# An attention layer on one core: the softmax shift's rest on another engine, q and k loaded in three runs of rows, and the first band edges ahead of the output

## The reference

```python
x = x + attention(layernorm(x))     # 16 heads of 16, Wq, Wk, Wv, Wo
x = x + ffn(layernorm(x))           # ternary weights, a low-rank side path, relu squared
# attention:
attend = (abs(i - j) <= 128) | (i < 1) | (j < 1)
logits = where(attend, q @ k.T / 4, -inf)
out = softmax(logits) @ v @ Wo.T
```

## Time and profile before

| | |
|---|---|
| time, median of 3 runs | 1136.79 us (1133.0 to 1143.12) |
| the profiled execution: its own time, its span | 1132.38 us, 1130.5 us |
| busy over the span: TensorE, VectorE, ScalarE, GpSimd | 93%, 83%, 68%, 61% |
| TensorE's mean granted clock | 0.984 of full |
| exps (1591), 512 | 394.4 us busy, 140.9 idle before, 137.8 of it for score banks |
| tiles read (1644), 1024 | 402.2 us busy, 66.6 idle before, 62.7 of it for TensorE |
| band edges (1417), 256 | 270.5 us busy, 10.6 idle before |
| outputs (1456), 64 | 39.8 us busy, 122.9 idle before, 100.3 of it for the reciprocal |
| value products (1529), 2816 | 223.0 us busy, 23.9 idle before, 20.2 of it for the band edges |
| score products (1507), 5632 | 242.1 us busy, 19.4 idle before, 13.5 of it for the shift rows' transfer |

### The profile page before, as it was taken

The page is one execution under the profiler, slowest core; times in us unless marked ns, Lnnn a source line. Parts: engine busy times, 40 slices in busy tenths (PEclk is TensorE's granted clock), DMA queues, the critical chain, the costliest instruction groups (busy, mean ns, idle before and its releaser), DMA issues. The chain is left out here.

```text
span 1130.5 us, 40183 instructions
## 1 busy us (share of the span) xinstructions
PE 1056.5 (93%) x16091; PEld 789.1 (70%) x16091; DVE 939.7 (83%) x3233; ACT 772.8 (68%) x1321; POOL 690.4 (61%) x916
## 2 busy tenths in 40 slices
PE   9999998998989989898998999889999999999998
PEld 8888884455555555455555566458888888898887
DVE  7899856997989988897888999657888788878885
ACT  7999984676777777776777777745655456545654
POOL 3665558486778877876787877853443344433443
PEclk9999998899999999999999999989999999999999
DMA  6999898457556566564566664230411122112201
GB/s 202 298 303 281 268 252 202 110 130 149 132 134 145 113 133 159 129 141 107 133 147 143 149 143 103 59 115 1 129 58 57 57 87 81 57 57 66 67 20 38
DMA packets 189707, 145.69 MB, mean 129 GB/s; under 512 B 61240, under 2 KB 189264, under 8 KB 189520
## 3 DMA queue, kind: packets, MB, share of 16 engines
q1 hardware_dynamic: 189520, 143.12, 49.0%
HBM read 91.32 MB, written 50.95 MB: 126 GB/s over the span
## 5 line engine op out<-in xcount | busy, mean ns | idle before, releaser
L1591 ACT ACTIVATE a_weights<-e_psum 128x1024 f32<-128x1024 f32 (+1 forms) x512 | 394.4, 809 | 140.9 <-PE e_psum L1507 137.8
L1644 DVE CUSTOM_DVE_ANT_0 a_masked<-e_psum,band 128x290 f32<-128x290 f32 (+8 forms) x1024 | 402.2, 444 | 66.6 <-PE e_psum L1482 62.7
L1417 POOL TENSOR_SCALAR_AFFINE_SELECT a_weights<-a_weights 128x1024 f32<-128x1024 f32 x256 | 270.5, 1091 | 10.6 <-ACT a_weights L1591 10.5
L1869 POOL TENSOR_TENSOR f_square<-f_relu 128x512 f32<-128x512 f32 x128 | 146.2, 1143 | 209.4 <-ACT f_relu L1858 192.1
L1507 PE MATMUL e_psum<-e_q,e_k 128*32 128x256 bf16 (+2 forms) x5632 | 242.1, 281 | 19.4 <-DMA e_q<-a_shift 13.5
L1482 PE MATMUL e_psum<-e_k,e_q 96*32 96x290 bf16 (+2 forms) x4096 | 233.9, 290 | 14.6 <-DVE a_max L1644 6.9
L1529 PE MATMUL e_psum<-a_weights,a_v 128*17 128x384 f32 (+2 forms) x2816 | 223.0, 398 | 23.9 <-POOL a_weights L1417 20.2
L1507 PEld LDWEIGHTS e_psum<-e_q,e_k 128*32 128x32 bf16 x5632 | 129.9, 97 | 115.1 <-ACT a_weights L1591 39.1
L1482 PEld LDWEIGHTS e_psum<-e_k,e_q 96*32 96x32 bf16 x4096 | 113.2, 98 | 86.1 <-DVE a_max L1644 54.9
L1825 PE MATMUL e_psum<-w_w_t,f_square_hi 128*128 128x256 f32 x512 | 129.4, 287 | 5.7 <-DVE f_square_lo L1915 5.7
L1827 PE MATMUL e_psum<-w_w_t,f_square_lo 128*128 128x256 f32 x512 | 126.7, 282 | 0.0
(11 more groups left out here) (218 smaller groups left out, 1898.1 us busy)
## 6 DMA issues: line engine op xcount, KB each, us to landing
k_parts<-p_k_parts SPq DMA_DIRECT2D x48, 258.0 KB, 4.2
e_k<-k_parts SPq DMA_DIRECT2D x64, 193.5 KB, 3.6
e_k<-k_parts SPq DMA_DIRECT2D x192, 64.5 KB, 3.3
q_parts<-p_q_parts SPq DMA_DIRECT2D x48, 256.0 KB, 4.9
e_q<-q_parts SPq DMA_DIRECT2D x64, 192.0 KB, 3.7
e_q<-q_parts SPq DMA_DIRECT2D x192, 64.0 KB, 3.3
v_ones<-p_va SPq DMA_DIRECT2D x16, 544.0 KB, 5.4
p_x<-in_x SPq DMA_DIRECT2D x16, 512.0 KB, 6.2
```

The source lines that it names most:

```text
L1417: pool.affine_select(out=blocks, in_=blocks, compare_op=ALU.is_ge, fill=0.0, base=0, pattern=[[0, NQ // 2 * HEAD_COLS // P // CUT_STEP], [ ...
L1591: act.activation(pe_w[:, us.upar, lo:hi], score[c % 2][:], ACT.Exp).then_inc(s_exp, 1)
L1644: dve.tensor_tensor_reduce(out=masked[:, place + lo:place + hi], in0=bank[:, lo:hi], in1=band[:, lo:hi], scale=1.0, scalar=NEG, op0=ALU.ad ...
L1869: pool.tensor_tensor(sh.r2[:, j % 4, :], sh.r[:, j % 4, :], sh.r[:, j % 4, :], ALU.mult).then_inc(self.s_sq, 1)
```

## The change

- **Rest.** The difference between the maxima and their HIGH is taken by GpSimd, as the first thing in a second step, instead of by VectorE behind tile 4. It is no longer negated: q's three rows now hold the maximum itself, and k's rows of ones hold minus ones.
- **HIGH** is copied by ScalarE ahead of the step's first exp instead of behind it.
- **LOW** comes ahead of key 0's products on GpSimd instead of behind them.
- **Band edges.** The first two (the first half of the weights, both sides) come ahead of the output, the other two stay behind it.
- **q and k.** In DRAM the part is now the outermost dimension, ahead of the row within a head, so that runs of rows in a tile's order of slots are single transfers: `RUNS` has three for each tile (48, 32 and 16 rows) where there were four (48 and three of 16). For that the columns of the turned Q and K weights are ordered otherwise, and they are copied in halves.

```diff
@@ -47,7 +47,7 @@
 
-TWO_ONES = float(np.array([0x3F803F80], np.uint32).view(np.float32)[0])
+MINUS_ONES = float(np.array([0xBF80BF80], np.uint32).view(np.float32)[0])
 DMA = 16
@@ -56,7 +56,7 @@
 SLOTS = 6
-SINGLES = ((MID, HIGH, HIGH), (HIGH, MID, HIGH))
+RUNS = (((0, 3), (0, 2), (0, 1)), ((0, 3), (1, 3), (2, 3)))
 SLOT_ROWS = SLOTS * HD
@@ -272,6 +272,16 @@
     sem[1] = start + 3
+
+
+def head_columns(w, m):
+
+    return w[:, m * P:(m + 1) * P].rearrange("p (d i h) -> p i h d", d=HD, h=NQ)
+
+
+def head_rows(w, m):
+
+    return w.rearrange("p (h m i d) -> p m i h d", h=NQ, m=KT, d=HD)[:, m]
 
@@ -394,12 +404,12 @@
                 if q := at(LP):
-                    rows = q_dram[bass.ds(q.g, 1)].rearrange("a i d s h m t -> (a i d) s (h m t)")
+                    rows = q_dram[bass.ds(q.g, 1)].rearrange("a s d i h m t -> (a d i h) s (m t)")
                     for part, done in ((HIGH, s_high), (MID, s_mid), (LOW, s_low)):
                         sp.wait_ge(done, q.g * 4 + KT)
                         sp.dma_start(rows[:, PLACE[0][part]], q_parts[:, q.par, :, PLACE[0][part]]
                                      ).then_inc(s_qout[q.par], DMA)
-                    rows = k_dram[bass.ds(q.g, 1)].rearrange("a i d s h m t -> (a i d) s (h m t)")
+                    rows = k_dram[bass.ds(q.g, 1)].rearrange("a s d i h m t -> (a d i h) s (m t)")
                     sp.wait_ge(s_gap, q.g * KT + KT)
@@ -598,9 +608,9 @@
                 for k in range(KT):
-                    ins = act.activation(wt_hi[:, w, k].rearrange("p (i d h) -> p i h d", d=HD, h=NQ),
-                                         w_bank[w][:, k * D:(k + 1) * D].rearrange("p (h i d) -> p i h d", d=HD, h=NQ),
-                                         ACT.Copy)
+                    for m in range(KT):
+                        ins = act.activation(head_columns(wt_hi[:, w, k], m), head_rows(w_bank[w][:, k * D:(k + 1) * D], m),
+                                             ACT.Copy)
                 ins.then_inc(s_whi, 1)
...
@@ -1220,7 +1230,7 @@
 
-    LOADS = 1 + len(SINGLES[0])
+    LOADS = len(RUNS[0])
 
@@ -1233,15 +1243,15 @@
         m, i = u.hq // 2, u.hq % 2
-        places = [(1, k_dram[b * GB + c:b * GB + c + 1, i, :, :, :, m], self.kt[u.hq][:, :, c * KGT:(c + 1) * KGT])
+        places = [(1, k_dram[b * GB + c:b * GB + c + 1, :, :, i, :, m], self.kt[u.hq][:, :, c * KGT:(c + 1) * KGT])
                   for b, c in self.chunks_of(u)]
-        places += [(0, q_dram[u.g:u.g + 1, i, :, :, :, m], self.qw[u.q])]
+        places += [(0, q_dram[u.g:u.g + 1, :, :, i, :, m], self.qw[u.q])]
         for which, src, dst in places:
-            src = src.rearrange("a d s h t -> (a d) s h t")
-            sp.dma_start(dst[0:PARTS * HD], src.rearrange("d s h t -> (d s) h t")).then_inc(landed, DMA)
-            for n, part in enumerate(SINGLES[which]):
-                sp.dma_start(dst[(PARTS + n) * HD:(PARTS + n + 1) * HD], src[:, PLACE[which][part]]
-                             ).then_inc(landed, DMA)
+            src, first = src.rearrange("a s d h t -> (a s d) h t"), 0
+            for start, stop in RUNS[which]:
+                count = stop - start
+                sp.dma_start(dst[first * HD:(first + count) * HD], src[start * HD:stop * HD]).then_inc(landed, DMA)
+                first += count
 
...
@@ -1420,12 +1430,20 @@
                 um, us, uo = at(L_SHIFT), at(L_SCORE), at(L_OUT)
+                if um and um.last:
+                    pool.wait_ge(s_high, um.pair + 1)
+                    wait(pool, s_low, um.pair)
+                    pool.tensor_tensor(rest[:], mt[:], shift[:, um.ppar, HIGH, :], ALU.subtract).then_inc(s_rest, 1)
                 if uo:
                     pool.wait_ge(s_turned, uo.n + 1)
                     pool.tensor_tensor(den[:, uo.upar], turned[:, uo.upar, :, HD], p0[:, uo.p0], ALU.add
                                        ).then_inc(s_den, 1)
                     pool.tensor_tensor(num[:, uo.upar], turned[:, uo.upar, :, 0:HD], t0[:, uo.n % 3], ALU.add
                                        ).then_inc(s_num, 1)
+                if um and um.last:
+                    pool.wait_ge(s_mid, um.pair + 1)
+                    pool.tensor_tensor(shift[:, um.ppar, LOW, :], rest[:], shift[:, um.ppar, MID, :], ALU.subtract
+                                       ).then_inc(s_low, 1)
                 if us:
@@ -1437,16 +1455,15 @@
                         p0[:, us.p0].unsqueeze(2).broadcast_to([P, SUBS, HD]), ALU.mult).then_inc(s_t0, 1)
-                if um and um.last:
-                    pool.wait_ge(s_mid, um.pair + 1)
-                    pool.tensor_tensor(shift[:, um.ppar, LOW, :], rest[:], shift[:, um.ppar, MID, :], ALU.subtract
-                                       ).then_inc(s_low, 1)
                 if um:
                     pool.wait_ge(s_tile_read, um.n * TILES + TILES)
                     wait(pool, s_p0, um.n - 1)
                     pool.tensor_tensor(d0[:, um.upar].rearrange("p (t j) -> p t j", j=QUADS), key0_scores(um),
                                        mx[:, um.ppar, um.upar * TILES:(um.upar + 1) * TILES].rearrange("p (t j) -> p t j", j=QUADS), ALU.subtract
                                        ).then_inc(s_d0, 1)
+                if us:
+                    cut(us, 0, 0)
+                    cut(us, 0, 1)
                 if uo:
@@ -1458,8 +1475,6 @@
                         feed.norm.power(pool, Group(0))
-                    cut(us, 0, 0)
-                    cut(us, 0, 1)
                     cut(us, 1, 0)
...
@@ -1582,6 +1597,10 @@
                     feed.act_o_high(act, Group(1))
+                if um and um.last:
+                    act.wait_ge(s_m, um.pair + 1)
+                    wait(act, s_row[um.ppar], um.phalf * DMA * SHIFT_ROWS)
+                    act.activation(shift[:, um.ppar, HIGH, :], mt[:], ACT.Copy).then_inc(s_high, 1)
                 for c in range(CHUNKS):
@@ -1589,10 +1608,6 @@
                         act.activation(pe_w[:, us.upar, lo:hi], score[c % 2][:], ACT.Exp).then_inc(s_exp, 1)
-                    if um and um.last and c == 0:
-                        act.wait_ge(s_m, um.pair + 1)
-                        wait(act, s_row[um.ppar], um.phalf * DMA * SHIFT_ROWS)
-                        act.activation(shift[:, um.ppar, HIGH, :], mt[:], ACT.Copy, scale=-1.0).then_inc(s_high, 1)
                     if um and um.last and c == 2:
@@ -1626,12 +1641,6 @@
                 for j in range(TILES):
-                    if um and um.last and j == 4:
-                        dve.wait_ge(s_high, um.pair + 1)
-                        wait(dve, s_low, um.pair)
-                        dve.scalar_tensor_tensor(out=rest[:], in0=mt[:], scalar=-1.0,
-                                                 in1=shift[:, um.ppar, HIGH, :], op0=ALU.mult, op1=ALU.subtract
-                                                 ).then_inc(s_rest, 1)
                     if ux:
@@ -2068,8 +2077,8 @@
 def layer(nc, x, wq, wk, wv, wo, fast_b, w_fc, w_proj, u, v, gate, out):
-    q_dram = nc.dram_tensor("q_parts", [G, UPG // KT, HD, PARTS, NQ, KT, GT], BF16, kind="Internal").ap()
-    k_dram = nc.dram_tensor("k_parts", [G, UPG // KT, HD, PARTS, NQ, KT, KGT], BF16, kind="Internal").ap()
+    q_dram = nc.dram_tensor("q_parts", [G, PARTS, HD, UPG // KT, NQ, KT, GT], BF16, kind="Internal").ap()
+    k_dram = nc.dram_tensor("k_parts", [G, PARTS, HD, UPG // KT, NQ, KT, KGT], BF16, kind="Internal").ap()
     va_dram = nc.dram_tensor("v_ones", [N, VROW], F32, kind="Internal").ap()
```

14 lines of the change are left out of this document (7 added, 7 removed).

## The result

| | before | changed |
|---|---|---|
| time, median | 1137.92 us (4 runs, 1133.0 to 1143.12) | 1105.6 us (4 runs, 1103.48 to 1110.43) |
| ratio | | 0.9721, 95% interval 0.9665 to 0.9778 |
| profiled execution: time, span | 1132.38, 1130.5 us | 1110.43, 1108.7 us |
| the 58 steps of the loop | 493.41 us | 464.04 us |

The kernel became 2.8% faster, and 1104 was forecast. The profiled execution of the changed kernel is the slowest of its four. Timed again twice, beside new runs of the kernel before, the changed kernel had a ratio of 0.9718 (0.966 to 0.9777) and 0.9757 (0.97 to 0.9813).

A forecast was written before the change was run, and what follows sets the result against it. A cycle through GpSimd's band edges and VectorE's reciprocal was taken to set the 8.27 us step, late shift rows second. Terms -19.3 - 3 + 4 - 11 + 0.3 = -29.0 gave 1104 us, range 1076 to 1126 (8 in 10).

The forecast's parts named there:

- the ring: Attention loop: band edges, value products, VectorE's reciprocal, GpSimd's output, edges again; 8.27 us, said to set the step's length.
- The edges, -19.3 us: Attention loop: two of four edges leave the cycle, giving back TensorE's 19.3 us of waiting for edges; bounds 0 and -46.
- 7.81: Attention loop: TensorE's busy time per quiet step in us, taken as the next limit once the edges move.
- the first rival: Attention loop: TensorE's busy time is no floor, steps fall to 7.5 us; -53, 1081 us, chance 0.17.
- Low earlier and fewer transfers, -11 us: Shift rows into q: LOW a microsecond sooner, six transfers a unit instead of eight; 80% of 13.2 us saved.
- Now it is late for all three: SyncE in the kernel before: still issuing the odd unit's loads when the shift rows are ready; some 1.0 us a unit saved.
- At most two steps over 9 us, and no clock below full: Attention loop: a sign that would show the forecast right, long steps and lowered TensorE clock nearly gone.
- +0.3: Kernel's start: Q and K weights copied in twice as many halves, costing 0 to +1 us.
- Rest off VectorE, -3: Attention loop: rest moves to GpSimd, saving half of TensorE's 6.6 us wait for VectorE's reads; 0 to -6.6.
- HIGH ahead, +4: ScalarE in the loop: first exp waits for turned maxima and HIGH's copy, about 0.2 us in 29 steps; 0 to +5.
- The last rival: ScalarE: HIGH ahead of the first exp makes a new cycle, +43 us, sum +12, 1146 us; slower, chance 0.08.
- That the rows come late all the same: Shift rows: transfers queue on DMA engines, not SyncE, so only -18 us, some 1115 us; chance 0.14.

The follow-up runs named there:

- E: Kernel before with only the first two band edges moved ahead of GpSimd's output: 1130.2 us, ratio 0.9937.
- S: Kernel before with only the shift's chain changed (rest on GpSimd, HIGH ahead of the first exp, LOW ahead of key 0's products): 1134.97 us, ratio 0.9994.
- the paced kernel: Changed kernel with SyncE holding back every odd step's loads until that step's third exp: 1109.05 us, ratio 0.9732 to the kernel before.
- L: Kernel before with only q's and k's loads in three transfers per tile, the new DRAM layout and the weights' halves: 1129.01 us, ratio 0.9958.

## Why the prediction was right

1104 was forecast and 1105.6 came, in the range, and of the cases the likeliest. The mechanism of the ring was right. That the sum comes within 2 us is luck: the edges brought 12 us more than forecast, gaps and the stages around the loop, which had 0.3 us between them, took 14 back, and HIGH and the rest, +4 and -3, came to nothing that can be told.

**The edges, -19.3 us (bounds 0 and -46).** The ring was what held the step: with E in it, and only then, the median pair falls from 8.3 to 7.8. The step's new length was to be 7.8 to 7.9 and is 7.77. Reckoned by the quiet step the gain is 0.54 x 58 = 31 us, 12 more than I took. The mis-sized step is the one that took back "exactly what it waited": the forecast's own step of 7.8 to 7.9 us, from 8.28 to 8.31, would have given 22 to 30 us. And 7.81 was no floor: busy time in the last five steps fell from 39.05 us to 37.38, 7.48 a step. Some of that is 15 matmuls fewer in the window. Over the loop, with 11452 and 11445 matmuls, it fell from 448.52 to 439.17 us, by 2%, while the busy times of tiles, scores and values, each taken by itself, rose from 209.2, 218.8 and 201.9 to 213.3, 219.8 and 204.4 us. So by the profile's records matmuls of different groups overlap more, and the engine's busy time is no sum of work. That speaks for the first rival, which gave 7.5 a step; it didn't get there, and 7.67 with a quarter of the loads was the least that any kernel showed. (The Trainium skill, "Trainium Kernel Development and Optimization", Performance Expectations, calls matmul busy time a bad measure of how near the limit is, because matmuls are pipelined. The trace agrees: 9.35 us of it went away in the loop without less work. That the weight loads are the good one can't be seen here, they fill 24.45 of 38.51 us and are not the bound either.)

**Low earlier and fewer transfers, -11 us.** The waits for the shift rows went from 13.1 to 2.0 us, as forecast. But the term had two causes in it, and one of them was idle: the six transfers do it alone (1.0 us of waits without S, 0.7 with E), the earlier LOW does nothing for them once the ring is broken (19.6 us with E and S, 20.4 with E), and with the ring in place 8.3 against 13.1 in one trace each. "Now it is late for all three" read the earlier trace rows too simply: SyncE was through with the loads at 265.64, and LOW was done at 266.38. HIGH and MID had waited, and LOW's row, behind theirs, went 1.45 us behind LOW. Then it took 4.97 us to land, where 2.3 is the median of LOW's rows. LOW's forecast place, 3.8 us into the step, was right (3.74), and so was that MID limits it. What I didn't see is that the edges' move alone brings LOW there, 3.63 us with the old order of the shift's chain. And the forecast added the terms as if each stood for itself; alone the edges would have brought 7 us by the median instead of 19.

**What ate it.** Over 58 quiet steps there were 493.4 - 58 x 8.31 = 11.4 us of long steps before. Now there are 461.5 - 58 x 7.77 = 10.9 (mean of three traces). The rows' waits are gone and the loop keeps its long steps: six over 9 us in the profiled run and stretches with the clock at 0.50. "At most two steps over 9 us, and no clock below full" was wrong. In place of the rows' waits there are 8.3 to 10.8 us of gaps without a releaser. They were no term of mine. I had put the new layout at 0, and it is the layout's kernels that have most of them: the four traces with the old one have 0.7 to 5.4 us (mean 2.7), the eight with the new one and all bytes, the paced kernel aside, 5.5 to 12.1 (mean 8.8). Those with the old one lie behind v's issues as well, but are fewer.

**The layout otherwise.** Before the loop, too, something seems to be lost. GpSimd's first output comes at 226.4 to 229.1 us in four traces with the old layout (mean 227.9) and at 227.3 to 232.7 in ten with the new one (mean 230.1): 2.3 us for which I had +0.3, though the two ranges overlap. q's last transfer of 16 rows lands in 4.5 to 4.7 us at the median in all ten, and in the old layout's four traces the last one took 3.2; the stores of q, 5.6 us here and 4.9 before, have 5.0 to 6.0 and 4.9 to 5.5 in all traces and tell little. The queue's share is 51.9% for the same bytes where it was 49.0%. The landing of the changed kernel:

```profile
q_parts<-p_q_parts SPq DMA_DIRECT2D x48, 256.0 KB, 5.6
...
e_q<-q_parts SPq DMA_DIRECT2D x64, 64.0 KB, 4.5
```

**Rest off VectorE, -3.** VectorE's busy time in the loop is 422.75 us with E and L and 414.85 with S added, and TensorE waits 6.9 and 7.0 us for it. Worth nothing that shows. The reciprocal beside the edges was not lengthened, as forecast: 248 ns at the median, 253 at most.

**HIGH ahead, +4.** Nothing that can be told, see above.

The sum by three traces of the changed kernel: -31.9 us in the loop, +3.8 ahead of it, +1.4 behind it, -26.7, where the forecast said -29.0. Within the loop it is -31 for the ring, -11 for the rows' waits and 9 back in gaps. (The last rival's sum doesn't come out: its +43 with the other terms gives +10 to +14 and not +12, which changes nothing.)

**The rivals.** That the rows come late all the same, because transfers queue on the DMA engines and not on SyncE, is false for most of the waiting and true for the rest. With eight loads a unit and the edges moved, LOW's row was issued up to 3.9 us behind LOW; with six it was 0.6 at most in the profiled execution of the changed kernel, and the waits fell from 19.6 to 2.0 us, although LOW's rows then landed no sooner (3.1 us at the median in both, 2.3 before). What remains is the rival's: at the two longest waits, 0.99 and 1.02 us, the row was issued 0.2 us behind LOW and landed in 4.6 and 5.8. So it was in the kernel before at its longest wait, 2.64 us, where the row was issued 0.03 us behind LOW and landed in 5.6. (The Trainium skill, "DMA: Bandwidth & Descriptors", Issuing engines are not separate DMA queues, calls the issue time "usually small relative to the DMA itself". Here too one issue, some 0.5 us, is small beside a landing of 3.3. Two of eight issues less nevertheless take 13 and 18 us from the traces' loops once the ring is broken, and about 20 us from the medians, since what counts is what stands behind them in SyncE's order.) A ring through HIGH did not form: HIGH waits 11.7 us for the turned maxima in 27 pieces of 0.6 at most, where 1.1 a step was the point from which it decides.

## What to carry to other kernels

Two limits that lie close together pay only together: break the ring and the late transfer is in the way, mend the transfer and the ring still holds. So try the parts in pairs before dropping one that alone brings half a per cent. Where a small transfer is late, look first at what its issuing engine has still to issue, before making its data earlier. Take a busy engine's busy time as a floor only with care: TensorE's shrank by 2% over the loop when the waits about it went. And when gaps have no releaser, look in several traces at what was issued at a fixed time ahead of each.

## What the runs showed that was not expected

- TensorE stands for up to 3.2 us, often in the middle of a tile, with no semaphore to explain it. All 47 such gaps of 0.9 us or more begin 5.6 to 10.4 us behind the issue of a chunk of v, and in 44 of them the DMA engines' share was 0.92 to 1.26 in the 2 us before. A quarter of q's and k's bytes, with v whole, takes the gaps in the loop from some 10 us to 1.5. What TensorE lacks in them, its own instructions perhaps, no view shows; nor is it settled whether the order of rows in DRAM or the longer transfers bring more of them, since the new layout with four transfers wasn't tried.
- The same bytes in pieces of the same size cost the queue more in another layout: 51.9% against 49.0% of the span, in all traces with it 50.9 to 52.8, in those with the old one 49.0 to 50.1. Part of that is a shorter span: 49.0% of 1130.5 us is 554 us of all engines, 51.9% of 1108.7 is 575, so 4% more.
- The parts' gains are far from additive: 0.6 and 0.4% alone, 2.4% together.
